# First four score units of the next pass moved into the current loop body, bank plan of the second attention's head changed, step orders of two loops written out

## The reference, cut to what matters

```python
x = x + _L0_attn_a_ref(_layernorm(x), Wq, bq, Wk, bk, Wv, bv, rel_bias)    # 16 heads of 8, softmax(q k / sqrt(8) + bias) v
x = x + _L0_ffn_ref(_layernorm(x), sg, su, sd, rg, ru, rd, wr, rb)         # one shared expert + top 2 of 7, inner 352
x = x + _L0_attn_b_ref(_layernorm(x), qkv_proj, qkv_bias, out_proj, out_bias)
x = x + _L0_ffn_ref(_layernorm(x), sg, su, sd, rg, ru, rd, wr, rb)
```

## Time and profile before

| what | value |
|---|---|
| median of 3 runs | 2579.62 us (2575.34 to 2588.03) |
| the profiled execution | 2579.83 us, its span 2578.0 us |
| mean granted TensorE clock | 0.846 |
| PE busy | 2069.0 us (80%) |
| DVE busy | 1596.0 us (62%) |
| ACT busy | 1358.8 us (53%) |
| POOL busy | 881.0 us (34%) |
| HBM traffic | 65 GB/s over the span |

### The profile page before, as it was taken

The page is one execution under the profiler, slowest core; times in us unless marked ns, Lnnn a source line. Parts: engine busy times, 40 slices in busy tenths (PEclk is TensorE's granted clock), DMA queues, the critical chain, the costliest instruction groups (busy, mean ns, idle before and its releaser), DMA issues. The chain is left out here.

```text
span 2578.0 us, 51329 instructions
## 1 busy us (share of the span) xinstructions
PE 2069.0 (80%) x14166; PEld 1400.4 (54%) x14166; DVE 1596.0 (62%) x6106; ACT 1358.8 (53%) x2893; POOL 881.0 (34%) x953
## 2 busy tenths in 40 slices
PE   5789999999999999949999656767676676599995
PEld 3456666666666666626665444545545454366663
DVE  3477777777777777736555346565656655355552
ACT  3577888888888888715444332323223232154442
POOL 3111111111111111126777612222231313177776
PEclk8788888888888888869999867676777777699998
DMA  5100000000000000036777511101010100377774
GB/s 199 56 16 15 16 17 17 17 17 17 17 17 17 17 17 17 14 110 155 178 178 169 110 30 32 31 29 33 25 37 25 33 25 25 128 160 176 181 175 81
DMA packets 125947, 168.85 MB, mean 65 GB/s; under 512 B 17288, under 2 KB 93968, under 8 KB 125888
## 3 DMA queue, kind: packets, MB, share of 16 engines
q1 hardware_dynamic: 62400, 122.50, 15.0%
q0 software_dynamic: 51968, 37.26, 9.8%
q10 hardware_dynamic: 11520, 8.39, 1.2%
HBM read 111.96 MB, written 56.12 MB: 65 GB/s over the span
## 5 line engine op out<-in xcount | busy, mean ns | idle before, releaser
L1092 ACT ACTIVATE z<-z,nm 128x256 f32<-128x256 f32 x1024 | 440.2, 500 | 94.1 <-DVE nm L1342 93.8
L1342 DVE CUSTOM_DVE_ANT_0 z<-bank_S,big 128x256 f32<-128x256 f32 x1024 | 378.9, 420 | 166.8 <-PE bank_S L1615 127.8
L961 POOL DMA_INDIRECT sent<-rows,slots x256 | 249.2, 973 | 243.2 <-DVE slots L1425 167.1
L1502 DVE SCALAR_TENSOR_TENSOR both<-both,bank_E 128x512 f32<-128x512 f32 (+1 forms) x228 | 155.5, 682 | 227.1 <-ACT both L1162 226.7
L1031 POOL DMA_INDIRECT out_x<-yo,xs x152 | 236.1, 1553 | 119.8 <-ACT yo L1176 43.5
L1031 POOL DMA_INDIRECT x<-yo,xs x152 | 235.4, 1549 | 119.3 <-DMA x<-yo,xs 43.1
L946 POOL COPY seen<-seen 128x8 f32<-128x8 f32 x32 | 6.1, 189 | 720.2 <-DVE picked L1308 684.1
L1615 PE MATMUL bank_S<-kx,qx 32*128 32x256 f32 x1024 | 207.1, 363 | 34.8 <-DVE nm L1342 31.0
L1696 PE MATMUL bank_E<-xbh,w_gu 128*128 128x512 f32 (+1 forms) x342 | 182.3, 533 | 39.1 <-DMA w_gu<-w_split 26.5
L1615 PEld LDWEIGHTS bank_S<-kx,qx 32*128 32x128 f32 x1024 | 126.4, 207 | 118.3 <-DVE nm L1342 64.4
L1162 ACT ACTIVATE both<-bank_E 128x512 f32<-128x512 f32 (+1 forms) x228 | 137.8, 604 | 95.6 <-PE bank_E L1698 91.6
(11 more groups left out here) (215 smaller groups left out, 4421.5 us busy)
## 6 DMA issues: line engine op xcount, KB each, us to landing
w_gu<-w_split SPq DMA_DIRECT2D x76, 704.0 KB, 5.4
xs<-sent SPq DMA_DIRECT2D x76, 264.0 KB, 2.7
w_dn<-w_split SPq DMA_DIRECT2D x76, 192.0 KB, 5.3
w_split<-w_gu SPq DMA_DIRECT2D x7, 704.0 KB, 3.1
both<-in_w_raw SPq DMA_DIRECT2D x8, 544.0 KB, 4.7
xin<-in_x SPq DMA_DIRECT2D x16, 256.0 KB, 2.7
sent<-rows,slots POOLq DMA_INDIRECT x256
x<-xo ACTq DMA_DIRECT2D x16, 256.0 KB
```

The costliest lines, as they stand in the source:

```text
L961: pool.indirect_dma_start(out=sent, out_offset=bass.IndirectOffsetOnAxis(ap=slots[:, n:n + 1], axis=0), in_=rows[:, k, t, :], in_offset=No ...
L1092: last = act.activation(zt, zt, ACT.Exp, bias=nm[:, n % NM_RING, t:t + 1], scale=-1.0)
L1342: last = dve.tensor_tensor_reduce(z[:, n % Z_RING, t * SEQ:(t + 1) * SEQ], bank[s][:, t * SEQ:(t + 1) * SEQ], bias_a[:, h, P - P * t:P - P ...
L1502: dve.scalar_tensor_tensor(out=a, in0=a, scalar=1.0, in1=in_blocks(q)[0:m, :], op0=ALU.add, op1=ALU.mult).then_inc(ba_ready, 1)
```

## The change

It has three parts.

1. **Early units (A).** `EARLY` = 4: the steps `scores` and `probs` of units 0 to 3 of pass p+2 now belong to the body that holds the attention of pass p+1 (`of_next`, `steps_ahead`). `PT_RING` grows from 5 to 8, so that `probT` can hold them across the loop's edge.
2. **Banks of B's head.** `turn1` and `v` take bank E2, which only `bturn` used, `qk.0` bank S1 and `qk.1` bank O (`B_HEAD`). They no longer wait for the experts' banks, but for the scores that were in S1 and O. The uses are counted by `early`, `MID` and `late`.
3. **Orders written out.** `WRITTEN` gives the order of both loops' bodies for PE, ACT, DVE, POOL and SP, in place of the planner's.

```diff
-PT_RING = 5
+PT_RING = 8
+EARLY = 4
@@
-        "B": {"S0": 3, "S1": 2, "T": 3, "O": 2, "E2": 1, "Q0": 1, "Q1": 1, **CHAIN}}
+        "B": {"S0": 3, "S1": 3, "T": 3, "O": 3, "E2": 3, "Q0": 0, "Q1": 0, "Y": CHAIN["Y"],
+              "PY": 0}}
...
+def of_next(kind, step, n):
+
+    return step in AHEAD or kind == "A" and step in ("scores", "probs") and n < EARLY
...
+WRITTEN = {
+    "A": {
+        "pe": "scores.4 scores.5 turn2.0 scores.6 scores.7 mix.0 scores.8 probs.4 begin.0 logits.0 context.0 probs.5 "
...
+                "spread.3 probs.1 spread.4 probs.2 spread.5 spread.6 probs.3 spread.7",
...
+    "B": {
+        "pe": "bscores.0 bscores.1 turn2.0 bscores.2 logits.0 begin.0 bmix.0 up.0 bscores.3 bmix.1 gate.0 turn1.0 gate.1 "
+                "qk.0 rank.0 qk.1 bmix.2 bmix.3 gate.2 up.1 bturn.0 up.2 bout.0 down.0 down.1 down.2 v.0 end.0",
+        "act": "turn2.0 bscores.0 bscores.1 gate.0 route.1 turn1.0 gate.1 bscores.2 bscores.3 qk.0 qk.1 gate.2 bturn.0 sum.0 "
+                "v.0 end.0",
+        "dve": "bscores.0 bscores.1 begin.0 logits.0 bprobs.0 route.0 bprobs.1 route.1 norm1.0 norm1.1 norm1.2 norm1.3 "
+                "norm1.4 norm1.5 norm1.6 route.2 gate.0 route.3 route.4 bscores.2 bscores.3 gate.1 rank.0 bprobs.2 bprobs.3 "
+                "up.0 bmix.1 bmix.3 up.1 gate.2 up.2 bout.0 norm2.0 norm2.1 norm2.2 norm2.3 norm2.4 norm2.5 end.0 norm2.6",
...
+BESIDE.update({kind: written(kind) for kind in WRITTEN})
...
+    B_HEAD = ("S1", "O")
...
+    def early(p):
+        return 0 if p.first else -1
+
+    MID = 1
+
+    def late(p):
+        return 2 if p.last else 3
...
                 if step == "turn1":
                     pe.wait_ge(normed1, p.count(same(1), 1))
 
+                    if p.kind == "B":
+                        turn_rows(p, xn, "E2", early(p))
+                        return
                     if p.next(-2):
                         pe.wait_ge(emptied["Y"], use(p.next(-2), "Y", 3))
                     turn_rows(p, xn, "PY", 0)
                 elif step == "qk":
+                    if p.kind == "B":
+                        s = B_HEAD[n]
+                        pe.wait_ge(emptied["E2"], use(p, "E2", early(p)))
+                        next_use(p, s, early(p))
...
                 elif step == "v":
-                    next_use(p, "PY", 1)
                     wide = p.kind == "B"
+                    s, k = ("E2", MID) if wide else ("PY", 1)
+                    next_use(p, s, k)
```

More of the change, by code:

```diff
@@ L195, with needs_unit @@
 OWN = 0.06
+def needs_unit(eng, step, n):
+    if step == "scores":
+        if eng == "pe":
+            spreads = [(n < EARLY, ("act", "spread", n // 4 + k)) for k in range(2)] if n % 8 == 0 else []
+            return spreads + [back("scores", "dve", n, 2)]
+        if eng == "dve":
+            return [(True, ("pe", "scores", n)), back("probs", "pe", n, Z_RING)]
+        return [(True, ("dve", "scores", n))]
+    if eng == "pe":
+        return [(True, ("act", "scores", n)), back("probs", "act", n, 2)]
+    used = (n - PT_RING) % UNITS
+    return [(True, ("pe", "probs", n)), (n >= PT_RING or n < EARLY, ("pe", "mix", used // 4))]
 def needs_attention(kind, eng, step, n):
@@ L298, in needs_before @@
     if step in ("turn2", "twin", "keep") and eng in ("pe", "pool"):
-        return [("dve", "norm2", last)] + ([("dve" if kind == "A" else "act", "v", 0)] if step == "turn2" else [])
+        return [("dve", "norm2", last)] + ([("dve", "v", 0)] if step == "turn2" and kind == "A" else [])
     if step == "begin" and eng == "pool":
@@ L423, in one_round @@
                     t = (e,) + s
-                    if s[0] not in seen and all(w in done for w in needs[t]):
+                    name = (s[0], of_next(kind, *s))
+                    if name not in seen and all(w in done for w in needs[t]):
                         start = max([free[e]] + [done[w] + (hand_over if w[0] != e else OWN) for w in needs[t]]
@@ L440, in one_round, with first_order @@
     return out, done
-FIRST = {k: order(k, steps_ahead(k), []) for k in "AB"}
+def first_order(kind):
+    steps = steps_ahead(kind)
+    head, units = ([x for x in steps if (x[0] in AHEAD) == w] for w in (True, False))
+    a, b = order(kind, head, []), order(kind, units, [])
+    return {e: a[e] + b[e] for e in FLOW}
+FIRST = {k: first_order(k) for k in "AB"}
 ALONE = {k: order(k, steps_attention(k, True), []) for k in "AB"}
```

176 lines of the change are left out of this document (96 added, 80 removed), and 25 rows, old and new, of the table WRITTEN.

## The result

| | before | after |
|---|---|---|
| median (runs) | 2579.88 us (2575.34 to 2588.03, 4) | 2447.33 us (2439.13 to 2449.16, 4) |
| ratio to before | 1 | 0.948, 95% interval 0.945 to 0.951 |
| profiled execution, span | 2579.83, 2578.0 | 2449.16, 2447.4 |
| one body of A's loop | 64.87 us | 68.2 us |
| one body of B's loop | 44.3 us | 30.7 us |

The kernel is 132 us faster, where 218 us were forecast: the measured time lies above the range. And the halves came out in opposite directions. B saves 13.6 us a body, not 8.75. A, which was to save 6.87 us, costs 3.3 us more.

What follows compares the result with a forecast made beforehand. A was taken as bound by PE, a drain at the loop's edge and the slow clock, B by a chain of waits; 96 us from A plus 122 from B, off 2579.83, gave 2361 us, range 2310 to 2428.

Steps and rivals of the forecast that it cites:

- 44.30 - 9.85 + 1.1: B's body: today's period less the wait for the first `bscores`, plus the body's end, giving 35.55 us.
- 1.1 us for the body's end: B's body end: allowance for two more waits of DVE like that for `end`, one gained and one kept.
- the 3.8 us for `bout`: B's body: DVE's wait for `bout`, 3.8 us a body today, left in the forecast sum.
- Orders written out. They have no price of their own: Both loops: the written orders were only the places of the other parts and got no separate price.
- rival 3: B's loop becomes bound by PE at half clock, some 41 us a body; 2438 us in all; chance 0.08.
- The clock to stay at 1.0.: A's loop edge: with the gap ahead of `turn2` under 1 us, PE's clock holds 1.0; loop clock 0.97 or more.
- rival 2: A's clock still falls at the loop's edge: body 62.7 us, 2428 us in all; chance 0.11.
- since PE then has no gap longer than those that it has at full clock: A's edge: reason given for a steady clock; the full-clock piece holds it with 2.80 us idle of 50.02.
- my sum had 58.0: A's body: 57.1 us of PE at 94.4% density plus 0.9 us for the edge; 6.87 us less than before.
- Nothing is added or dropped: A's early units: the same 32 `scores` and `probs` per body, four of them for the next pass.
- 53.9 us of PE at full clock: A's body: PE's work at full clock, summed as 1.34 + 10.66 / 2 + 47.22.
- In A the experts' steps are spread more evenly, which I count at nothing: A's loop: the written order's more even spread of the experts' steps was priced at zero.

Runs made afterwards that it cites:

- warm: The changed kernel with 4 matmuls for nothing ahead of `turn2`'s wait and 8 behind `turn2` in A's loop; 2410.48 us, ratio 0.934.
- planned_paired_warm_2: planned_paired with 6 matmuls for nothing behind the last spread and 6 ahead of the first `mix`, in condition X; 2430.77 us, ratio 0.943.
- planned_paired: The changed kernel with the planner's order in A's loop and PE's `scores` in 16 adjacent pairs; 2368.99 us, ratio 0.919.
- paired_third: The changed kernel with written orders, PE's `scores` moved into 16 adjacent pairs on PE alone, in condition X; 2449.30 us, ratio 0.950.
- planned_paired_warm: planned_paired with 6 matmuls for nothing behind the last spread and 6 ahead of the first `mix`, in condition Y; ratio 0.944.
- b_alone_3: The changed kernel with only B's part (banks, written order), A's loop as in the kernel before, in condition Y; 2696.64 us, ratio 0.958.
- paired_again: The changed kernel with PE's `scores` in 16 adjacent pairs on PE alone, in condition Y; ratio 0.956.
- warm_paired: warm with PE's `scores` in adjacent pairs, in condition Y; ratio 0.961.

## Why the prediction was wrong

**B, wrong in size, right in direction.** The step that failed is the sum "44.30 - 9.85 + 1.1". The wait for the first `bscores` went, as said, and its 9.85 us were the right term. But I charged 1.1 us for the body's end and kept the 3.8 us for `bout`, while both waits nearly vanished: 4.8 / 13 = 0.4 us and 3.1 / 13 = 0.2 us remain. 9.85 + 3.4 + 0.9 = 14.2 us of DVE's waits went, its wait for `up` grew by 0.6 us a body (7.2 us in 13 bodies before, now 14.9), and the body lost 13.6. Nor would the banks alone have given the 9.85 us: without the written order 7.0 us of it come back as the wait for the third `gate`. "Orders written out. They have no price of their own" was wrong here, to the good, by 9.4 us a body. The clock in B rose from 0.72 to 0.90, and rival 3 (PE at half clock) did not occur. The fullest engine is DVE, with 26.8 us of work, which none of my cases named.

**A, wrong in direction.** Three steps.

*"The clock to stay at 1.0."* It fell as before, which is rival 2, and stayed at half for 17 us. I had noted that the fall at 652.75 came ahead of the long gap, and gave the rival 0.11. The gap ahead of `turn2` closed as forecast, to 0.27 us, but the clock again fell ahead of it, and PE got another gap behind it. So the step that failed is "since PE then has no gap longer than those that it has at full clock": it took the gap for the cause. The Trainium skill, TensorE: Matmul & The Clock Gate, section HAM oscillation, puts falls of the clock down to PE idling between bursts. This case's traces agree only in part: filling both gaps kept the clock at 1.0 in the last bodies of *warm*, but the falls themselves come behind stretches in which PE was busy 6.8 of 7.4 us, and 6.7 of 7.2 in planned_paired_warm_2. planned_paired comes near what rival 2 worked out, 62.7 us for A's body against 63.2 measured, though it is another order than the one that was forecast.

What the clock is worth without a filler one interval tells, the first of planned_paired, from the copy ahead of the loop to the next. It has 405 of the usual 413 groups of matmuls, a clock of 0.97, and takes 57.63 us, where my sum had 58.0:

```profile
135.45:193.08 57.63, 52.69 (x405) 34.42 (x406) 47.50 (x237) 48.74 (x108) 11.86 (x19) 0.97 0.07 20
```

It is one interval, at the way into the loop; the steady bodies never had it.

*"Nothing is added or dropped"*, the same matmuls and so the same 53.9 us of PE at full clock. The matmuls are the same, the time isn't: with the pairs of `scores` parted PE is busy 65.1 us a body in place of 59.1. By the three rows of the body above, its work at full clock is 1.59 + 14.99 / 2 + 48.55 = 57.6 us where the sum had 53.9. The half clock adds 14.99 / 2 = 7.5 us, which the sum had at nothing, and PE is idle for the other 3.1 of the 68.2 us. The Trainium skill, TensorEngine Tiling (Array Packing), section Key Properties, says that different tiles can load and multiply in parallel. By it a pair of 32-row units costs PE as much as one, and the trace agrees (0.43 us for two units or one, and 63 us in 14 bodies with 11 pairs less each); both orders could be read before the run, and I did not count who stands beside whom.

*"In A the experts' steps are spread more evenly, which I count at nothing."* This is the one that decides. planned_paired against paired_third prices the written orders of A at 5.0 us a body, 70 us in 14. PE's density did rise (98% in the full-clock piece, where I took 94.4%), but because PE's work grew. With the pairs together in paired_third the work fell again, and the density with it.

Beside these stands DVE's idle 2.40 us at the loop's turn. It is in the kernels with early units, and in none without; the two exceptions are planned_paired_warm and planned_paired_warm_2, where DVE waits at that place for the `scores` behind the fillers (up to 5.9 us in the second). The number of instruction packets moves with it: 33 in the kernels without early units, 98 in all with them. The DMA part of the page of after:

```profile
q14 instruction: 98, 0.80, 0.1%
```

65 more in 13 bodies are 5 each, and three of a body's five lie between 616 and 624 us, around the stall. That the packets and DVE's stall belong together is my reading from their place and number, argued and not shown. A kernel that shortens DVE's body alone wasn't tried.

In sum: A's body of 68.2 us is the 63.2 us of early units in the planner's order (rival 2 had 62.7) and 5.0 for the written orders. The early units bring at most 1.7 us in X, in the planner's order and together with three more pairs, where 6.87 were forecast. What stays open is which single place of the written orders costs most, what brings the clock down at the edge, and whether a steady body can keep it at 1.0 without a filler.

## What to carry to other kernels

When an order is rewritten, price the neighbours too: matmuls of 32 rows in different strips share their time when they are adjacent (0.43 us for two units or for one here), and busy time grows when they are parted. Then look at the other engines before putting them together again, since what PE saves can come back as waits on the engine that empties its banks. A filler for a gap has to be measured and cut to the gap: 5.6 us in gaps of 0.27 and 1.90 us paid for itself through the clock, 8 us in a gap of 2.6 us did not. Before a gap is called the cause of a fall of the clock, look whether the clock falls behind it or ahead of it. And a change that frees a chain (B's banks) may only hand the wait on until the order is changed with it.

## What the runs showed of the hardware

*Two conditions, one kernel.* In Y the kernel before takes 9% longer than in X. The trace of b_alone_3 shows where in B, with single instructions of DVE as long as in X (one subtraction of the maxima, L1469, takes 692 ns in both). While POOL issues the eight scatters of a pass, some 10 us, DVE and ACT stand still, with waits that the profile calls remote. The waits of b_alone_3 in 13 bodies of B, in Y:

```profile
DVE rec_b L1482 <- remote: 127.9, 13, 9.9
ACT both L1238 <- remote: 110.1, 13, 8.6
```

In X neither row exists. That is 9.8 us of a B body that is 11 us longer (41.8 against 30.7). Why X and Y differ I can't say. It also decides what a change is worth: with the written order and the pairs, a clock of 0.84 (paired_again) and one of 0.91 (warm_paired) both gave A bodies of 75.1 us there, from the fourth interval on.

*The clock can fall with PE nearly always busy.* In the changed kernel PE is busy 1.59 of the 1.60 us in which the clock falls, and 1.17 of the 1.80 us just ahead of them:

```profile
616.00:617.80 1.80, 1.17 (x8) 0.59 (x6) 1.49 (x11) 1.80 (x5) 0.00 (x0) 1.00 0.02 5
```

Then it is at half clock for 17 us, although it is busy 87% of that time (14.99 of 17.20).

*Instruction packets appear during a loop*, and an idle time that the profile puts down to "issue" appears with them, though DVE has as many instructions in its body as before (3173 in 13 bodies of either kernel).
